# Moving a few loads and one attention product in a two-block transformer kernel on one core

## What is computed

```
# first block (16 heads; its MLP weights are not used)
h  = sln(x, cond)                      # layer norm, scaled and shifted by the condition
q, k, v = h @ Wqkv.T + bqkv
out = (softmax(q k^T) / sqrt(512)) v   # per head
h1 = out @ Wp.T + bp + x
x  = sln(h1, cond) + h1
# second block (one head of 512)
h  = film(rmsnorm(x), cond)
x2 = x + softmax(Q K^T * 512**-0.5) V @ proj_w + proj_b
h  = film(rmsnorm(x2), cond)
y  = x2 + gelu(h @ mlp_w1 + mlp_b1) @ mlp_w2 + mlp_b2
```

## Time and profile before

| what | us |
|---|---|
| median of 3 runs (lowest, highest) | 1500.79 (1499.12, 1503.34) |
| the profiled execution, its own time | 1506.07 |
| span of the profiled execution | 1504.3 |
| PE busy in it | 1476.9 |
| DVE busy | 937.4 |
| ACT busy | 670.6 |
| POOL busy | 623.7 |

### The profile page before, as it was taken

The page is one execution under the profiler, slowest core; times in us unless marked ns, Lnnn a source line. Parts: engine busy times, 40 slices in busy tenths (PEclk is TensorE's granted clock), DMA queues, the critical chain, the costliest instruction groups (busy, mean ns, idle before and its releaser), DMA issues. The chain is left out here.

```text
span 1504.3 us, 24225 instructions
## 1 busy us (share of the span) xinstructions
PE 1476.9 (98%) x8712; PEld 1199.6 (80%) x8712; DVE 937.4 (62%) x1878; ACT 670.6 (45%) x2023; POOL 623.7 (41%) x544
## 2 busy tenths in 40 slices
PE   8999999999999999998999899999999999999999
PEld 5888888888887668776888678888888888888887
DVE  6777777777766676766767643674358433764354
ACT  4656565555645455555766432432225223432210
POOL 5756667676745547654856202211114102401001
PEclk9999999999999999998999999999999999999999
DMA  7222222322115435776653746535553555545432
GB/s 254 67 93 78 79 98 71 106 72 93 64 65 180 149 121 169 253 264 236 199 182 140 280 182 217 169 119 208 202 180 110 225 181 176 182 148 196 153 129 96
DMA packets 92793, 232.58 MB, mean 155 GB/s; under 512 B 9665, under 2 KB 17857, under 8 KB 87553
## 3 DMA queue, kind: packets, MB, share of 16 engines
q1 hardware_dynamic: 89216, 213.09, 41.3%
q10 hardware_dynamic: 3456, 17.93, 3.0%
HBM read 174.17 MB, written 56.82 MB: 154 GB/s over the span
## 5 line engine op out<-in xcount | busy, mean ns | idle before, releaser
L1326 ACT ACTIVATE pa<-bank,neg_max 128x128 f32<-128x128 f32 x512 | 181.8, 409 | 136.4 <-DVE neg_max L1737 136.4
L719 PE MATMUL bank<-w_hi,g_hi 128*128 128x512 f32 x512 | 200.7, 392 | 0.0
L720 PE MATMUL bank<-w_lo,g_hi 128*128 128x512 f32 x512 | 199.5, 390 | 0.0
L721 PE MATMUL bank<-w_hi,g_lo 128*128 128x512 f32 x512 | 199.3, 389 | 0.0
L1217 PE MATMUL bank<-op_hi,ring 128*128 128x512 f32 x448 | 176.0, 393 | 6.0 <-DVE u2p L2162 5.2
L1221 PE MATMUL bank<-op_hi,ring 128*128 128x512 f32 x448 | 175.3, 391 | 0.0
L1219 PE MATMUL bank<-op_lo,ring 128*128 128x512 f32 x448 | 175.3, 391 | 0.0
L2324 POOL TENSOR_TENSOR pa<-pa,rec 128x512 f32<-128x512 f32 x128 | 143.1, 1127 | 54.2 <-DVE rec L1760 54.0
L2296 POOL TENSOR_TENSOR xrc<-xrc,b 128x512 f32<-128x512 f32 x32 | 50.2, 1602 | 271.5 <-DMA xrc<-x_dram 271.5
L1587 ACT ACTIVATE sum<-sum,cols 128x512 f32<-128x512 f32 x128 | 92.1, 722 | 115.1 <-DVE sum L2162 115.1
L1326 ACT ACTIVATION_READ_ACCUMULATOR pa<-bank,neg_max 128x1 f32 x512 | 127.2, 248 | 0.0
(11 more groups left out here) (263 smaller groups left out, 3553.7 us busy)
## 6 DMA issues: line engine op xcount, KB each, us to landing
ring<-w_dram SPq DMA_DIRECT2D x32, 1792.0 KB, 7.5
rows<-st_dram SPq DMA_DIRECT2D x32, 512.0 KB, 4.4
hid_dram<-sum SPq DMA_DIRECT2D x64, 256.0 KB, 2.2
hid<-hid_dram SPq DMA_DIRECT2D x64, 256.0 KB, 2.7
w_dram<-w_parts ACTq DMA_DIRECT2D x8, 1792.0 KB, 6.3
xa<-xt_in SPq DMA_DIRECT2D x32, 256.0 KB, 4.1
xra<-xt_in SPq DMA_DIRECT2D x32, 256.0 KB, 2.8
x_dram<-h SPq DMA_DIRECT2D x32, 256.0 KB, 2.0
```

What stands on the lines that cost most here:

```text
L719: nc.tensor.matmul(dst, w_hi, a_hi, start=start, stop=False)
L720: nc.tensor.matmul(dst, w_hi, a_lo, start=False, stop=False)
L721: return nc.tensor.matmul(dst, w_lo, a_hi, start=False, stop=stop)
L1326: last = nc.scalar.activation(pa[:, j, m, :], scores_bank[j][:, m * P:(m + 1) * P], ACT.Exp, bias=neg_max[:, j * C + m:j * C + m + 1], acc ...
```

## The change

Four edits, all of order. One: in stage B, from the second group on, SP issues token loads 2 and 3 of the next group ahead of residual load 2 instead of behind it. Two: W2 pieces 2 to 7 are loaded by SP instead of ACT, two at the beginning of each of `p = 1, 2, 3`, ahead of that piece's `store_hid`; the wait for the buffer goes with them. Three: `attend_b(7, 3)` stands after product 3 instead of after product 1, and DVE's copies for it (`copy_ptb`) behind `low_first(2)` and `low_first(3)` instead of ahead of them. Four: POOL's last addition of a bias (`add_bias` for tile 31) waits for the last `op_lo`.

```
-                for b in range(GB - 1):
+                for b in range(2):
                     load_bxr(g, b)
                 if not first:
                     for b in range(2, GB):
...
+                load_bxr(g, 2)
+                if not first:
                     store_x2(g - 1, GB - 1)
                 load_bxr(g, GB - 1)
...
             def load_w2(i):
+                wait(sp, w2_lo_made, i - 1)
                 sp.dma_start(stage_w2[i % 2][:], w2_rows[i]).then_inc(w2_in[i % 2], 16)
...
+                    if first and 0 < p < GB:
+                        load_w2(2 * p)
+                        load_w2(2 * p + 1)
                     store_hid(n, 1)
                     store_hid(n, 0)
...
-                        if first and p == 0 and i == 1:
+                        if first and p == 0 and i == 3:
                             attend_b(NG - 1, GB - 1)
...
-                if 1 <= i < NP - 1:
-                    act.wait_ge(w2_lo_made, i)
-                    nc.scalar.dma_start(stage_w2[(i + 1) % 2][:], w2_rows[i + 1]).then_inc(w2_in[(i + 1) % 2], 16)
...
-                    if b < GB - 1 or last:
+                    if b < GB - 1:
                         copy_ptb(g, b)
...
                 if last:
                     low_first(2)
                     low_first(3)
+                    copy_ptb(g, GB - 1)
                 dve.wait_ge(brec, GB * g + GB - 1)
                 residual_b(g, GB - 2)
...
                         for i in range(GB):
                             rest_first(i)
+                        pool.wait_ge(op_lo_made, 2 * GB)
                     add_bias(GB * g + b, b, xrb, cb1, bxr_in[b], loaded(g + 1), bxr)
```

## The result

The changed kernel takes 1492.68 us (median of 4 runs, 1491.07 to 1492.97), the kernel before on the same chip 1502.07 us (4 runs, the three of the table and one more, 1499.12 to 1505.23). The ratio is 0.9935, with a 95% interval of 0.9912 to 0.9958: faster by 9.4 us. The forecast was 1491 us, in a range of 1485.5 to 1497.5.

The account below looks back on a forecast made before the run. PE, busy 1476.9 of 1504.3 us, bounds the kernel; order can return only waits and low clock. 3.1 + 0.85 + 4.38 + 3.1 - 0.3 = 11.1 us; with clock halved 9.2, giving 1491.6; forecast 1491 us, range 1485.5 to 1497.5.

Parts of the forecast that it names:

- Edit two, sized 4.38 us and 3.1 us of clock: Stage C: earlier W2 loads remove PE's waits of 2.62 and 1.76 us and the low clock behind the first.
- The fourth rival: Stage C: W2 piece 3 stands behind a ring load in SP's queue, comes after 859; 1495.2 us, chance 0.07.
- Edit one, sized 3.1 us: Stage B: earlier token loads shorten PE's waits by 0.8, 1.6 and 0.7 us in groups 1, 2 and 3.
- Group 3: ... I take 0.7 of 7.51: Stage B, group 3: token loads gain one queue place and one transfer, 0.5 to 1.2 us; most of the wait stays.
- Group 3's bound: Stage B, group 3: residual loads issued in a row directly ahead of the token loads, so gain only 0.5 to 1.2 us.
- the chain rival: Stage B waits are a chain; all 11.86 us go with the low clock: 23.5 us gained, 1477 us, chance 0.08.
- Edits three and four, sized 0.3 us lost: Where stages B and C meet: 0.60 gained, a longer `u2p` wait opens, W2 piece 1 comes later; 0.3 us lost.
- The slower rival: Stage B's last store lands late, delaying W2 piece 1 and SP's work behind it; 1505.5 us, chance 0.04.
- the prediction's limit of about 842.5: Start of stage C: once W2 piece 1 comes later than about 842.5, every further us stops PE for one.
- The clock, counted half (2.0 us): Low clock behind waits in group 1 and at W2 piece 3: 3.95 us expected back, half counted for the median.
- the 0.85 us: Stage B, group 1: with the wait at 1.3 us low clock may stay away; half of 1.7 us counted.

Follow-up runs that it names:

- late W2: Changed kernel with W2 pieces 3, 5 and 7 loaded by SP behind gelu stores, ring load and residual loads: 1500.46 us, ratio 1.0003.
- residual behind: Changed kernel with DVE's last residual of stage B behind the second sum `u2p` of n = 0: 1492.2 us, ratio 0.9929.
- attention back: Changed kernel with edit three undone (last attention product after product 1, copies ahead of the low halves), edit four kept: 1492.36 us, ratio 0.9929.
- W2 alone: Kernel before with only edit two (W2 pieces 2 to 7 loaded by SP ahead of the gelu stores): 1496.24 us, ratio 0.9966.
- attention alone: Kernel before with only edits three and four (attention product after product 3, copies later, POOL's addition later): 1500.3 us, ratio 0.9997.
- the two experiments on it: Changed kernel with token loads ahead of all residual loads: 1484.17 us, 0.9875; changed kernel with x_late loads moved from group 2 to group 3: 1485.16 us, 0.9879.

## Why the prediction was right, step by step

The sum came out within 1.1 us: 1492.68 us against the 1491.6 worked out and the 1491 forecast. Part of that is luck, since the trace it was read from was no usual one, and errors went both ways. The single edits give 2.7, 5.1 and 0.5 us by their ratios, 8.3 together, against 9.4 (6.3 to 13.2) for the whole change, so no interplay between them shows.

**Edit two, sized 4.38 us and 3.1 us of clock: right, from a trace with large values.** Both waits are gone in the whole change and with this edit alone; alone it gave 5.1 us (2.9 to 7.5), between the waits and waits plus clock. The three traces without it (before, edit one alone, edits three and four alone) have 4.38, 2.56 and 4.07 us of these waits, and 3.1, 1.7 and 1.7 us of low clock behind the first. Piece 3 was issued at about 839.3 (SP's two W2 loads span 3.43 us from 836.28 and the second takes 0.4) instead of 849.55 and was there before ACT asked. The fourth rival, that the load comes too late behind a ring load, did not come: in the early place it stands behind one without harm. In the late place such a load took as long on SP's queue as on ACT's (9.1 and 9.6 us). The Trainium skill's rule (DMA: Bandwidth & Descriptors, "Queues, rings and completion order") is not refuted by that. But the advantage that the prediction drew from it for ACT's queue, that a W2 load could pass the ring load there, does not show: before, it landed 1.8 us behind the ring load that was issued 0.5 us ahead of it.

**Edit one, sized 3.1 us: right for groups 1 and 2, one term not shown.** The five kernels that have edit one and otherwise nothing in stage B (changed, alone, late W2, residual behind, attention back) against the three without it (before, W2 alone, attention alone):

| group | without edit one | mean | with edit one | mean | gain | foreseen |
|---|---|---|---|---|---|---|
| 1 | 2.09, 2.13, 1.40 | 1.87 | 1.46, 0, 1.02, 1.01, 1.11 | 0.92 | 0.95 | 0.8 |
| 2 | 2.26, 3.60, 2.06 | 2.64 | 1.01, 1.25, 0.98, 1.00, 0.98 | 1.04 | 1.6 | 1.6 |
| 3 | 7.51, 3.10, 4.41 | 5.01 | 5.86, 5.41, 6.02, 6.71, 5.52 | 5.90 | -0.9 | 0.7 |

Groups 1 and 2 gained what was worked out. The step "Group 3: ... I take 0.7 of 7.51" is not borne out: without the edit this wait goes from 3.10 to 7.51 in traces that differ in nothing there, and the one trace that I had held the largest. The changed kernel's 5.86 looks like a gain only beside that trace. The table's three gains add up to 1.7 us, those of groups 1 and 2 alone to 2.5; the edit's time alone, 2.7 us (0.8 to 4.8 by its interval), fits either and 3.1 too.

**Group 3's bound: read too narrowly.** I wrote that in group 3 "nothing but one place and one transfer is gained", and against the chain rival that its loads were issued in a row. Both are true, but the first of the row had itself waited for a slow store. The largest wait of stage B was open to an order change, just not to this one: each of the two experiments on it brought the ratio from 0.9935 to 0.988, nearly as much again as the whole change. The chain rival had the right object for the wrong reason.

**Edits three and four, sized 0.3 us lost: right for edit three, not shown for edit four.** 0.60 and 0.78 have become 0.29 and 1.50, 0.4 us more, against 0.2 worked out for this place. DVE's residual in front of `u2p` is the cause (taken away, so is the wait). But the 0.60 that edit four was to help with was a matter of one trace: the two others without edits three and four wait 0.94 and 0.78 us in all here, so the loss beside them is 0.85 and 1.0. The slower rival did not come: W2 piece 1 made no wait of PE in the changed kernel, where ACT stood 1.62 us for it instead of 0.62. How much of this is hidden, which no row told, the traces together do tell. ACT stood 1.81, 1.94, 2.04, 2.13, 2.23 and 2.32 us for this piece in six of them, and PE then 0.34, 0.46, 0.59, 0.66, 0.74 and 0.83 us: ACT may stand some 1.5 us, and every further one stops PE. Put on the trace of before (841.68 - 0.62 + 1.5 = 842.6), that bears out the prediction's limit of about 842.5. (This rival's time is 1505.3, not 1505.5: 1500.79 + 4.5.)

**The clock, counted half (2.0 us): right in direction, its size not settled.** Low clock did not come behind group 1 in the changed kernel, but it also stayed away in the kernel with edit two alone, behind an unshortened wait of 2.13 us, where the kernel before had it behind 2.09. So for group 1 alone the 0.85 us is not shown. Groups 1 and 2 together do show something: in each of the three traces without edit one, the wait of one of the two is followed by low clock (1.7, 2.4 and 1.7 us lost), in none of the five with it. The halving rested on the profiled execution of before, 5.3 us above its median. An estimate from the means of the traces without and with each edit is: 2.5 us for the waits of groups 1 and 2, 3.7 for those for W2, 0.8 lost where the stages meet, and 1.9 and 2.2 us of clock, 9.5 in all, beside 9.4 in the times. So the clock may well have given 4 us and the waits less than the 7.2 counted; the interval of the times (6.3 to 13.2) cannot tell.

## What to carry to other kernels

The larger stalls of the bounding engine began here with one small load that was issued late, because of its place in the list of the engine that issues it. List for each such load when its buffer is free and when it is issued, and move it ahead of every neighbour that waits for something else; that was worth most of 19 us here, and no cost of the queue showed. When a product is moved into a gap, look at what stands between its reader and the next thing that engine owes: the gap came back longer. And do not price a wait from one trace: the waits for transfers changed from trace to trace, and so did an overlap of two engines that looked like a cause.

## What was not expected of the hardware

The wait of group 3 went from 3.10 to 7.51 us between traces with identical instructions in that stage (and once, with 4.41, another of 0.85 opened in group 4), while with edit one in place group 2 stayed between 0.98 and 1.25 in five traces. In group 3 a 256 KB store took 14.1 us to land beside two W1 stores (15.8 before); the median of all loads and stores of `x_dram` from 590 to 850 us was 3.6 us.

Whether the clock goes low behind a wait is not told by the wait's length alone. These windows of the kernel with edit two alone start at the ends of waits of 2.13 and 3.60 us, the next ones, of the kernel with edits three and four alone, at those of 1.40 and 2.06:

```profile
612.30:617.00 4.70, 4.70 (x28) 4.12 (x29) 3.82 (x11) 4.28 (x12) 4.53 (x4) 1.00 0.43 116
647.30:652.00 4.70, 4.70 (x18) 4.31 (x19) 4.38 (x11) 3.71 (x11) 4.53 (x5) 0.50 0.48 131
```

```profile
611.80:616.00 4.20, 4.19 (x25) 3.74 (x26) 3.87 (x11) 3.87 (x12) 4.03 (x4) 1.00 0.48 129
645.30:649.30 4.00, 4.00 (x17) 3.68 (x18) 3.82 (x11) 3.67 (x11) 3.83 (x4) 0.57 0.45 136
```

A wait of 2.13 us was followed by full clock, one of 2.06 by the 1.2 GHz level for most of 4 us; before, 2.26 us had none (1.00 from 647.73 to 652) and 2.09 had it.
